# The last five gate operations of each chunk and layer: from GpSimd to VectorE

## What is computed

```python
x = x + _L0_cond_ref(x, cond_1024, ...)      # experts, layer 0
x = x + _L1_cond_ref(x, cond_1024, ...)      # experts, layer 1
x = x + _L2_cond_ref(cond_1024, x, W, b, alpha)
x = x + _L3_cond_ref(x, cond_1024, mask, ...)

# experts: the gates of the two chosen experts of each row
s = sigmoid(concatenate([xf, tf]) @ router_W)
_, topk_idx = top_k(s + router_bias, K)
s_sel = take_along_axis(s, topk_idx, axis=1)
denom = s_sel.sum(axis=1, keepdims=True)
gates = where(denom > 1e-09, s_sel / (denom + 1e-09), 1.0 / K)

# recurrence, one step
gate = sigmoid(h @ Wh.T + z_t @ Wz.T + b)
h = tanh(h * leak + gate * z_t)
```

## Time and profile before

| | |
|---|---|
| median of 3 runs | 534.01 us (532.18 to 534.34) |
| the profiled execution's own time | 533.74 us |
| its span | 531.9 us |
| PE busy | 484.1 us (91%) |
| DVE busy | 367.8 us (69%), 1631 instructions |
| ACT busy | 265.8 us (50%) |
| POOL busy | 27.5 us (5%), 92 instructions |
| granted TensorE clock, mean | 0.962 of 2.4 GHz |

### The profile page before, as it was taken

The page is one execution under the profiler, slowest core; times in us unless marked ns, Lnnn a source line. Parts: engine busy times, 40 slices in busy tenths (PEclk is TensorE's granted clock), DMA queues, the critical chain, the costliest instruction groups (busy, mean ns, idle before and its releaser), DMA issues.

```text
span 531.9 us, 13709 instructions
## 1 busy us (share of the span) xinstructions
PE 484.1 (91%) x4714; PEld 323.6 (61%) x4714; DVE 367.8 (69%) x1631; ACT 265.8 (50%) x1072; POOL 27.5 (5%) x92
## 2 busy tenths in 40 slices
PE   4898998899998999999998878999997999999995
PEld 2676676566676766767764335566654566666662
DVE  5876888888887878888787688977432855455501
ACT  3432644534445355554455654465659344454471
POOL 7010100000001000010000000000000000000000
PEclk9999998998998999989999968999999799999997
DMA  8400000000000000000000000000000000000000
GB/s 312 175 0 2 2 2 1 2 1 3 2 2 0 2 1 2 2 1 2 2 1 2 1 2 1 2 2 2 11 11 1 21 1 3 2 1 22 1 2 20
DMA packets 4915, 8.36 MB, mean 16 GB/s; under 512 B 496, under 2 KB 3824, under 8 KB 4720
## 3 DMA queue, kind: packets, MB, share of 16 engines
q1 hardware_dynamic: 4416, 7.23, 3.8%
q10 hardware_dynamic: 432, 0.27, 0.2%
HBM read 6.44 MB, written 1.05 MB: 14 GB/s over the span
## 4 chain that ended last, share of the span: by engine, by line
PE 73%; ACT 11%; DVE 10%; issue 5%; DMA 1%; ACTq 0%; DVEq 0%
PE ybk L796 14%; PE hid L942 11%; PE ybk L919 6%; PE cbk L964 5%; PE cbk L961 4%; PE hid L897 3%; PE hid L906 3%; PE hid L852 2%; PE hid L782 2%; DVE vbk L1273 2%; PE hid L855 2%; PE hid L901 2%; PE hid L844 2%; ACT hhi L720 2%; ACT d L708 1%
## 5 line engine op out<-in xcount | busy, mean ns | idle before, releaser
L942 PE MATMUL hid<-xsp,up 128*128 128x256 f16 x672 | 97.7, 287 | 3.1 <-DVE lg L1081 1.3
L796 PE MATMUL ybk<-hg,down 128*128 128x256 f32 x352 | 97.0, 399 | 1.6 <-DVE hg L1145 0.8
L708 ACT ACTIVATE d<-cbk 128x8 f32<-128x8 f32 x256 | 45.7, 179 | 103.0 <-PE cbk L965 101.1
L961 PEld LDWEIGHTS cbk<-hhi,wh 128*128 128x128 bf16 x768 | 44.9, 98 | 56.6 <-ACT hhi L720 48.0
L1191 DVE TENSOR_REDUCE wm<-hid 128x2 f32<-128x256 f32 (+2 forms) x107 | 58.8, 553 | 28.7 <-PE hid L855 27.1
L720 ACT ACTIVATE hhi<-vbk 128x8 f16<-128x8 f32 x255 | 45.1, 177 | 59.5 <-DVE vbk L1273 59.4
L1273 DVE TENSOR_TENSOR_SCAN vbk<-d 128x16 f32<-128x16 f32 x256 | 50.4, 197 | 35.0 <-ACT d L708 31.0
L961 PE MATMUL cbk<-hhi,wh 128*128 128x8 f16 x768 | 58.0, 170 | 13.7 <-ACT hhi L720 12.3
L942 PEld LDWEIGHTS hid<-xsp,up 128*128 128x128 f16 x672 | 61.4, 101 | 14.4 <-issue 2.0
L698 ACT ACTIVATE hb<-hid,att 128x512 f32<-128x512 f32 x71 | 48.6, 688 | 41.1 <-PE hid L906 41.0
L796 PEld LDWEIGHTS ybk<-hg,down 128*128 128x128 f32 x352 | 59.8, 190 | 8.0 <-DVE hg L1150 1.7
(11 more groups left out here) (170 smaller groups left out, 738.2 us busy)
## 6 DMA issues: line engine op xcount, KB each, us to landing
qz<-up_in SPq DMA_DIRECT2D x3, 512.0 KB, 7.2
kp<-maskr_in SPq DMA_DIRECT2D x1, 1024.0 KB, 11.1
out_dram<-silu SPq DMA_DIRECT2D x4, 256.0 KB, 2.4
x<-x_in SPq DMA_DIRECT2D x7, 128.0 KB, 8.3
down<-down_in SPq DMA_DIRECT2D x1, 768.0 KB, 9.2
att<-att_in SPq DMA_DIRECT2D x1, 751.0 KB, 9.3
down<-down_in SPq DMA_DIRECT2D x1, 640.0 KB, 6.6
qz<-up_in SPq DMA_DIRECT2D x1, 256.0 KB, 3.9
```

The costliest lines, as they stand in the source:

```text
L708: nc.scalar.activation(d1[:, t % 2, :, 0], cbk[c % 2][:, o:o + B], ACT.Tanh, scale=0.5).then_inc(gate_th, 1)
L796: m = pe.matmul(ybk[l][:, 0:n], D(l, "w2" if shared else "e2", e * f + i), hg[:, hg_of[made] % NHG, i * n:i * n + n], start=first and i == ...
L942: m = pe.matmul(into, up[:, pw, a:a + P], x_part(c, l, px, slice(0, n)), start=j == 0, stop=j == 2)
L961: pe.matmul(pre, wh3[:, i, :], hhi[:, t % 2, :], start=False, stop=True, skip_group_check=True)
```

## The change

The five gate operations of `RG` are issued by VectorE. `RG` becomes a unit of DVE with a planned cost of 1000 ns, is in `HALVED` (two operations ahead of the scan, three behind) and stands in a slot like the others. GpSimd keeps its setup work at the start alone. The waits on GpSimd's semaphore in `GT` and `RS` become waits on DVE's own counter or go. The operations, their shapes and their data stay.

```diff
-add(("RG", c, l), 0, 0, 0, False, (("RC", c, l), "dve", "pool"))
-add(("GT", c, l), 60 * k, 0, 60 + n, True, (("RG", c, l), "pool", "pe"),
+add(("RG", c, l), 0, 0, 1000, False, (("RC", c, l), "dve", "dve"), *([(("GT", c - 1, l), "pe", "dve")] if c else []))
+add(("GT", c, l), 60 * k, 0, 60 + n, True, (("RG", c, l), "dve", "pe"),
...
-                    link(tts(gr[:, 0:k, :], sg[:, l, 0:k, :], wide(rcp2[:, l, 0:k]), ALU.mult))
-                    link(tts(gr[:, 0:k, :], gr[:, 0:k, :], wide(zer2[:, l, 0:k]), ALU.add))
-                    link(tts(gr[:, 0:k, :], gr[:, 0:k, :], pick[:, l, 0:k, :], ALU.mult))
-
-                    link(nc.gpsimd.tensor_copy(g2[:, l, 0:k, 0:E], gr[:, 0:k, :]))
-                    tts(g2[:, l, 0:k, E:2 * E], gr[:, 0:k, :], g2[:, l, 0:k, 0:E], ALU.subtract).then_inc(gates_made, 1)
...
+                elif kind == "RG":
+
+                    _, c, l = key
+                    k = CHUNKS[c] * B // P
+                    wide = lambda a: a.rearrange("p (k o) -> p k o", o=1).broadcast_to([P, k, E])
+                    if half != 1:
+                        dve.wait_ge(dve_done, nth["dve", ("RC", c, l)])
+                        if c:
+                            dve.wait_ge(pe_done, nth["pe", ("GT", c - 1, l)])
+                        link(tts(gr[:, 0:k, :], sg[:, l, 0:k, :], wide(rcp2[:, l, 0:k]), ALU.mult))
+                        link(tts(gr[:, 0:k, :], gr[:, 0:k, :], wide(zer2[:, l, 0:k]), ALU.add), wait=False)
+                    if half != 0:
+                        dve.wait_ge(dve_link, chain[0])
+                        link(tts(gr[:, 0:k, :], gr[:, 0:k, :], pick[:, l, 0:k, :], ALU.mult))
+                        link(nc.vector.tensor_copy(g2[:, l, 0:k, 0:E], gr[:, 0:k, :]))
+                        i = tts(g2[:, l, 0:k, E:2 * E], gr[:, 0:k, :], g2[:, l, 0:k, 0:E], ALU.subtract)
...
-HALVED = ("GT", "YL", "SA", "SB", "M", "YE", "O", "RS", "RD", "RC", "KP", "QP", "A", "V", "X", "TR")
+HALVED = ("GT", "YL", "SA", "SB", "M", "YE", "O", "RS", "RD", "RC", "RG", "KP", "QP", "A", "V", "X", "TR")
```

More of the change, by code:

```diff
@@ L114, in plan @@
             for r, (a, b) in enumerate(half):
-                add(("R", c, l, r), 190 * (b - a), 0, 130, True, *x, *([(("RG", c - 1, l), "pool", "dve")] if c else []))
+                add(("R", c, l, r), 190 * (b - a), 0, 130, True, *x, *([(("RG", c - 1, l), "dve", "dve")] if c else []))
             add(("RT", c, l), 0, 220, 0, False, (("R", c, l, len(half) - 1), "dve", "act"))
@@ L333, in plan @@
     steps = {at: t for t, at in step_slot.items()}
[L335 to L339, removed]
     return parts, nth, steps, bank_of, before, hg_of, hb_of, n_slots
@@ L468, in build @@
         x_split = sem("x_split")
-        gates_made = sem("gates_made")
-        pool_link = sem("pool_link")
         consts = sem("consts")
@@ L758, in unit @@
                     k = CHUNKS[c] * B // P
-                    pe.wait_ge(gates_made, nth["pool", ("RG", c, l)])
+                    pe.wait_ge(dve_done, nth["dve", ("RG", c, l)])
                     for i in range(k):
@@ L1087, in unit @@
                     if half != 1:
-                        if c:
-                            dve.wait_ge(gates_made, nth["pool", ("RG", c - 1, l)])
                         tsc(sg[:, l, 0:k, :], th[:, l, 0:k, :], 0.5, 0.5, ALU.mult, ALU.add)
```

## The result

The changed kernel took 542.85 us (median of 4 runs, 541.19 to 545.46), the kernel before 534.13 us on the same chip. The ratio on record is 1.0175, with a 95% interval of 1.0135 to 1.0215; the two medians alone give 1.0163. A second series of six runs gave 542.39 us and a ratio of 1.0165 (1.0137 to 1.0192). The change costs 8.7 us. The profiled execution took 541.19 us, the lowest of the four, with a span of 539.4. The forecast was 5.2 us more, 539.0 us, with 542.6 as its upper end.

What follows compares the result with a forecast made beforehand. The recurrence's loop through PE, ACT and DVE, with a floor of 1.18 us a step, was taken as the bound. Terms 0.9 + 1.4 + 2.4 - 0.6 + 0.4 + 0.7 = +5.2 us gave 539.0 us, range 535.2 to 542.6.

Steps and rivals of the forecast that it cites:

- The crowded gaps: DVE's two gaps per step: units over 0.40 us behind the scan or 0.43 ahead delay the loop; +3 to +8, chance 0.62.
- `RG` alone: Ten recurrence slots holding only this unit: 0.49 us behind the scan against room for 0.40, 0.09 each, +0.9 us.
- `RG` with `R`: Three shared recurrence slots: 0.45 us too much ahead of the scan twice, 0.48 behind it once, +1.4 us.
- whole `RD`: Newly paired in four recurrence slots, 0.37 us too much ahead of the scan, 0.40 behind: +1.5 us.
- whole `RS`: Crowded recurrence slots: one behind a scan before, now two and one ahead, 0.41 us each behind: +0.8 us.
- the deduction of 0.6 us: First 200 steps: some crowded-gap costs fall on steps where PE was late already, only the larger counts: -0.6 us.
- The lead: Ahead of step 0: later `SB` and `RD` delays against PE work moved out; +0.7 us (-1.5 to +2.5).
- The clock: Half-clock stretches: 0.15 us lost per us at half clock; a new order moves them, plus or minus 1 us.
- The forecast's own signs: Expected profile: first 200 steps 262 to 263 us, lead about 47, DVE busy 14 us more.
- rival 2: Hidden anyway: crowded steps are late by PE or ACT already, lead gains; +0.6 to +2.4, 535 us, chance 0.22.
- rival 3: Faster: GpSimd's gate operations had held VectorE up in the recurrence; 529.4 us, chance 0.04.
- Rival 4: Worse: PE becomes the bound, all 1.8 us moved is paid, lead delays 2.5; +9.0, 543 us, chance 0.12.

Runs made afterwards that it cites:

- before_fill: The kernel before plus extra matmuls of zeros in the 22 slots up to slot 256 where PE had little to do; 529.69 us, ratio 0.992.
- after_fill: The changed kernel plus extra matmuls of zeros in 23 light slots of its order and 12 in the lead; 534.11 us.
- fill: The changed kernel plus 33 extra matmuls, 12 in the lead and the rest in slots 42, 43, 83, 84, 144 and 145; 537.03 us, ratio 1.0068.
- fill_less_lead: The kernel `fill` without its 12 extra matmuls in the lead; 537.96 us, ratio 1.0070 against the kernel before.
- after: The changed kernel itself, gate operations moved from GpSimd to VectorE against the kernel before; 542.85 us, ratio 1.0175.
- order_only: The changed kernel's order of all other units, with the five gate operations back on GpSimd; 541.29 us, ratio 1.0154 against the kernel before.
- ops_only: The kernel before in its own order, with the gate operations on VectorE three slots behind RC, not planned for; 538.06 us, ratio 1.0084.
- fill_less_late: The kernel `fill` without its six extra matmuls in slots 144 and 145; 538.13 us, ratio 1.0078 against the kernel before.
- ops_fill: The order of the kernel before with the gate operations on VectorE, plus the same extra matmuls as `before_fill`; 533.70 us, ratio 1.0003.

## Why the prediction was wrong, point by point

*The crowded gaps* were right, in place and size. `RG` alone was forecast at 0.09 us and took 0.08 to 0.09. `RG` with `R` was forecast at 0.45 to 0.48 and took 0.46 to 0.47. Steps with a whole `RD` (12, 54, 67 and 71) were to take 1.5 to 1.6 and took 1.51 to 1.55. A whole `RS` in steps 45, 130 and 153 took 1.59, 1.74 and 1.57, forecast 1.6. The steps with `RG` and `R` took 1.69 to 1.82 in all, where 1.6 was expected, since they took 1.22 to 1.35 without `RG` and not 1.19. Ten groups alone were too many by one or two: in steps 74 and 181 ACT's own unit made the step late (1.39 us with or without `RG`), which the deduction of 0.6 us stood for. The 200 steps at nearly full clock took 256.34 us in `before_fill` and 259.98 in `after_fill`, 3.6 us more. The forecast was 0.9 + 1.4 + 2.4 - 0.6 + 0.4 = 4.5. So the terms for the steps were 0.9 us too high together. The unfilled kernels differ by 6.24 us there, and the rest of that is not gaps.

*The lead* was forecast at +0.7 us and took +1.84 (+1.65 in the second profile). The mechanism was there: PE waited 1.77 us for `SB` behind the two conversions. With the lead filled it is +0.03 in `fill` (against the kernel before) and +0.8 in `after_fill` (against `before_fill`), so at full clock the term of 0.7 was not too small. The rest is the half-clock stretch behind this wait, 1.6 us (`fill_less_lead` against `fill`). One wait I had not seen: the last of the `WH` units now stands behind `YE` of chunk 0, and PE waited 1.15 us for it ahead of step 0:

```profile
46.73 0.67 PE L775 MATMUL cbk<-x,rec 128*128 128x256 f32 x2 [1.15 <-DVE hlo L1004]
```

*The clock* is the step that failed: "A new order moves these stretches, by plus or minus 1 us." I took its price, 0.15 us for each us at half clock, from one stretch of the attention, multiplied it with the time at half clock in the old order, and left its sign open. The runs showed a price that depends on what lies in the stretch. The kernel before has only `E` products in its three stretches behind empty slots. Such steps took 1.41 to 1.44 us, 0.22 to 0.25 over their 1.19, and one with `GT` besides 1.72 instead of 1.28. The six matmuls of an `E` take 0.6 us longer at half clock, and most of that found room in the step. The changed order has `Y` products in two of its stretches among the steps. Steps 4, 105 and 106, with a `Y` and an `M`, took 2.41, 2.36 and 1.66 us, 1.09, 1.16 and 0.37 over the same steps in `fill`: a `Y` and an `M` fill 1.09 us of a step at full clock, and there was no room for twice that.

By the same steps the half clock cost 3.8 us in the changed kernel (against `fill`) and 1.6 in the one before (against `before_fill`), and 1.6 more in the lead of the changed one alone. That is 5.4 us for 20.4 us at half clock against 1.6 for 13.7, 0.26 and 0.12 for each, and it makes 3.8 of the 7.4 us by which the two spans differ. A second count gives the same: lead and first 200 steps together grow by 8.1 us from the kernel before to the changed one (304.32 to 312.40), and by 4.4 from `before_fill` to `after_fill` (302.47 to 306.90). In the timed runs the difference of 8.7 us shrinks to 4.4 when both are filled, good to some 1.5 us. So the forecast of 5.2 was about the part that remains at full clock, and a little under half of the loss was the clock's, where the forecast had plus or minus 1 us. In the 200 steps all three changed kernels (`after`, `order_only` and `ops_only`) lost more before filling than after (6.2, 5.6 and 3.3 us against 3.6, 2.0 and 2.1), so here the clock went one way. The forecast's own signs in the unfilled profile were off accordingly: 264.3 us for the 200 steps instead of 262 to 263, a lead of 48.1 instead of 47, and DVE busy for 11 us more instead of 14.

The Trainium skill, TensorE: Matmul & The Clock Gate, What's actually happening, says of this that activity releases the throttle. The runs agree as far as extra matmuls at light places took stretches away (20.4 us at half clock ahead of step 200 in the changed kernel, 6.8 in `fill`).

*The rivals.* That it is hidden anyway (rival 2) falls, since the gaps came at full price. (Its terms add up to +0.6 to +2.2 us, not +2.4.) That GpSimd had held VectorE up (rival 3) falls: `hlo` has a mean of 166 ns with GpSimd's gate operations in the recurrence and 165 without, and `ops_only` lost 4.3 us. The contention that was found went the other way, VectorE's conversions holding GpSimd up in the lead. Rival 4 named 543 us, the right number, for a reason that the runs do not bear out: at nearly full clock the 200 steps grew by 3.6 us and not by the 6.5 that it needs there.

*What stays open*: which light place brings which stretch (`fill_less_late`), the gaps of DVE without a wait, and whether `ops_fill` costs more than its 3.3 us. That an order with the operations on VectorE could match `before_fill` was not tried.

## What to carry to other kernels

In a loop of small steps through several engines, cost a moved group by the gap in which it lands: here 0.40 us behind the scan and 0.43 ahead of it, every tenth beyond which lengthened the step by a tenth, though VectorE was idle for a sixth of the time. A new order also changes where the matmul engine has little to do, and what it works on when its clock falls; look for both, since a step that PE nearly filled already lost up to 1.16 us at half clock, one with room left 0.25. Filling light slots with matmuls that change nothing made even the kernel before 0.8% faster.

## What the hardware showed unexpectedly

The clock fell though PE was not idle for long: in the lead of `fill_less_lead` it had worked 1.49 us of the 3.5 us ahead of the fall, with 1.99 us as its longest wait, and in the recurrence of the kernel before each of three stretches had a single slot without a unit ahead of it. A fourth such slot, 158, had none behind it in either profile. Most stretches came at the same places of the program in both traced executions of one kernel, and 33 matmuls of 128x256 took 5.4 us off the changed kernel. Two gate operations of GpSimd took 1.13 and 1.20 us instead of 0.20 and 0.22 while VectorE converted weights, and VectorE's conversions took no longer for it (2.49 us there and in the changed kernel, where GpSimd was idle).
